# Tasks beside gathered in every second round, up to three in a row, in the bank beside and the first score's two banks

## What is computed

```python
latent_kv = x @ w_kv_down          # 256 -> rank 128
kv = latent_kv @ w_kv_up           # -> keys and values of 16 heads of 64
q = (x @ w_q).reshape(Bx, Tx, 16, 64)
att = jnp.einsum('bqhd,bkhd->bhqk', q, k) * scale
att = jnp.where(causal, att, -jnp.inf)
att = jax.nn.softmax(att, axis=-1)
y = jnp.einsum('bhqk,bkhd->bqhd', att, v)
return y.reshape(Bx, Tx, HD) @ w_out
```

## Time and profile before

| | |
|---|---|
| device time, median of 3 runs | 2116.73 us (2112.48 to 2118.43) |
| span of the profiled execution | 2113.7 us |
| PE busy, share of the span | 1984.7 us, 94% |
| DVE | 1337.2 us, 63% |
| ACT | 1097.9 us, 52% |
| POOL | 1425.9 us, 67% |
| granted clock of TensorE, mean | 0.980 |

### The profile page before, as it was taken

One profiled execution on the slowest core, in us unless ns is written; L12 is line 12 of the kernel. 1 busy time (PEld: TensorE's weight loads), 2 busy tenths in 40 slices (PEclk: granted clock), 3 DMA queues, 4 the chain that ended last, 5 costly groups with the idle time before them and its releaser, 6 DMA issues.

```text
span 2113.7 us, 35206 instructions
## 1 busy us (share of the span) xinstructions
PE 1984.7 (94%) x12886; PEld 1240.9 (59%) x12886; DVE 1337.2 (63%) x2728; ACT 1097.9 (52%) x2236; POOL 1425.9 (67%) x812
## 2 busy tenths in 40 slices
PE   8997788999999999999989999999999999999898
PEld 6775454555655555555555655555555555555466
DVE  7786555576656666666665657576756575656443
ACT  5775543455545454545455444545445445444585
POOL 1333225778687878787857687868786878687822
PEclk9998899999999999999999999999999999999999
DMA  3000000000000000000000000000000000000001
GB/s 124 1 1 1 0 7 13 13 19 10 13 18 16 13 19 12 19 10 19 13 12 17 12 20 11 17 12 20 11 18 11 20 11 18 11 14 11 26 26 60
DMA packets 29243, 37.01 MB, mean 18 GB/s; under 512 B 6928, under 2 KB 20368, under 8 KB 29072
## 3 DMA queue, kind: packets, MB, share of 16 engines
q1 hardware_dynamic: 29072, 34.76, 5.4%
HBM read 30.02 MB, written 4.46 MB: 16 GB/s over the span
## 4 chain that ended last, share of the span: by engine, by line
PE 63%; DVE 14%; POOL 12%; ACT 6%; issue 4%; DMA 1%; POOLq 0%; ACTq 0%; SPq 0%; DVEq 0%
PE heads_out L918 16%; POOL acc L1416 10%; PE beside L723 9%; PE scores L723 7%; PE two_heads L874 7%; PE scores L897 4%; PE scores L903 4%; PE scores L899 4%; PE scores L901 4%; DVE part_max L1112 3%; ACT prob L1331 2%; PE two_heads L723 2%; PE beside L929 2%; PE heads_out L723 1%; DVE wQK_lo L1073 1%
## 5 line engine op out<-in xcount | busy, mean ns | idle before, releaser
L1416 POOL TENSOR_TENSOR acc<-acc,prob 128x1024 f32<-128x1024 f32 (+3 forms) x512 | 1017.9, 1988 | 195.4 <-ACT prob L1331 140.1
L1331 ACT ACTIVATE prob<-scores 128x512 f32<-128x512 f32 (+3 forms) x1280 | 579.4, 539 | 649.2 <-PE scores L903 289.0
L1112 DVE TENSOR_REDUCE part_max<-two_heads 128x2 f32<-128x1024 f32 x384 | 469.3, 1222 | 280.5 <-PE two_heads L874 279.7
L918 PE MATMUL heads_out<-prob,V 128*64 128x512 f32 (+3 forms) x2560 | 544.4, 547 | 0.0
L1109 DVE CUSTOM_DVE_ANT_0 two_heads<-two_heads,mask 128x128 f32<-128x128 f32 (+3 forms) x512 | 242.0, 514 | 180.4 <-PE two_heads L874 180.4
L874 PE MATMUL two_heads<-k_hi,q_hi 64*128 64x512 f32 (+3 forms) x1280 | 274.1, 424 | 62.8 <-DVE part_max L1112 30.6
L918 PEld LDWEIGHTS heads_out<-prob,V 128*64 128x64 f32 x2560 | 156.7, 137 | 232.4 <-issue 209.6
L874 PEld LDWEIGHTS two_heads<-k_hi,q_hi 64*128 64x128 f32 x1280 | 120.6, 184 | 256.6 <-issue 133.4
L897 PE MATMUL scores<-q_hi,k_hi 64*128 64x512 f32 (+3 forms) x1280 | 236.1, 364 | 0.8 <-DVE k_lo L1100 0.5
L903 PE MATMUL scores<-neg_max,sel 64*128 64x512 f32 (+3 forms) x1280 | 235.6, 362 | 0.0
L901 PE MATMUL scores<-q_lo,k_hi 64*128 64x512 f32 (+3 forms) x1280 | 235.5, 362 | 0.0
(11 more groups left out here) (301 smaller groups left out, 2898.7 us busy)
## 6 DMA issues: line engine op xcount, KB each, us to landing
rden<-rden_rows SPq DMA_DIRECT2D x128, 128.0 KB, 2.9
X<-u SPq DMA_DIRECT2D x8, 512.0 KB, 8.7
out<-X SPq DMA_DIRECT2D x8, 512.0 KB, 2.9
wQK_raw<-wQuery SPq DMA_DIRECT2D x16, 192.0 KB, 3.1
wO_raw<-wOut SPq DMA_DIRECT2D x16, 128.0 KB, 2.8
wV_raw<-wValue SPq DMA_DIRECT2D x8, 128.0 KB, 2.9
den<-den_rows SPq DMA_DIRECT2D x64, 4.0 KB
rden_rows<-den SPq DMA_DIRECT2D x64, 4.0 KB, 1.3
```

Source lines behind the costliest of these rows:

```text
L918: made = pe.matmul(heads_out[head(h), x0:], V[vn % NVS][:, tt, p % 2, head(h)], prob[step % NPROB][:, h, x0:], start=t == 0, stop=t == TPB ...
L1112: made = ve.reduce_max(part_max[:, t, :, c:c + 1], two_heads[:, :, 0:width], AX.X)
L1331: ac.activation(prob[step % NPROB][:, h, x0:], bank(task, h)[:, x0:], ACT.Exp).then_inc(empty(task, h)[0], 1)
L1416: po.tensor_tensor(total[:, :, x0:], total[:, :, x0:], new[:, :, x0:], ALU.add).then_inc(acc_ok, 1)
```

## The change

In each round PE's tasks beside were one from any that is open (bank 7), then, in a round with no diagonal step, one more that is due within 8 steps (bank 0), and in rounds with a diagonal step and no denominators one more behind the weighing. Now the rounds alternate. In those with s % 4 == 2 up to three are taken in a row, in banks 7, 0 and 1: any, then one due within 16 steps, then one due within 8. In those with s % 4 == 0 only one that is overdue by two steps or more. None is taken behind the weighing any more. The two projections of a unit are due two steps earlier than they were. What is computed, and by which instructions, stays as it is.

```diff
             if kind == "two_parts":
-                fillers.extend([(s + 2, s + 4 + half, ("project", ready[0][1][1], half)) for half in range(2)])
+                fillers.extend([(s + 2, s + 2 + half, ("project", ready[0][1][1], half)) for half in range(2)])
...
-            filler(10 ** 6)
-            diagonal = not steps[s:s + 2] or any(t >= TPB * UNITS[idx][2] for idx, t in steps[s:s + 2])
-            if not diagonal:
-                self.side_bank = 0
-                filler(s + 8)
+            if s % 4:
+                for n, self.side_bank in enumerate((7, 0, 1)):
+                    filler((10 ** 6, s + 16, s + 8)[n])
                 self.side_bank = 7
+            else:
+                filler(s - 2)
             while self.at < goal - 1:
                 maximum()
...
             due("two_parts")
             due("scale_out")
-            if not due("denominators") and diagonal:
-                filler(s + 8)
+            due("denominators")
```

## The result

The changed kernel takes 2141.78 us (median of 4 runs, 2139.57 to 2143.72), the kernel before, on the same chip, 2114.61 us (4 runs, 2111.7 to 2118.43). The ratio is 1.0134, with a 95% interval of 1.0116 to 1.0152: slower, by 27 us. The forecast was 34 us slower, in a range of 2124 to 2182. The profiled execution of after has a span of 2138.3 us at a mean granted clock of 0.982.

A forecast was written before the change was run, and what follows sets the result against it. PE was taken as the bound, busy 94% of the span. Lost 36 + 33 + 2 = 71, won 22 + 9 + 2 + 3 = 36: +35 us on 2116.7, giving 2151.7, rounded 2151; range 2124 to 2182.

The forecast's parts named there:

- Step 5: Phases 22 and 30: demanded turned maxima and the next task both take bank 7, so PE waits; 33 us lost.
- the forecast's sign: Bank 7 clash would show as L723 waiting for ACT's `neg_max` some 30 times at 1.1 to 1.2 us.
- Step 4: First round of a unit, phases 0, 4, 12, 24: without a task beside, PE idles before the next maximum; 36 us lost.
- Step 2: Phase 6: key gets bank 0, so the denominators no longer wait for bank 7; 9 us won.
- Step 3: Phase 36: no projection behind the weighing, so the next maximum's reduction isn't held back; 2 us won.
- Step 1: Rounds with tasks beside: fewer groups, each costing 0.19 us beyond its products; 22 us won.
- Step 6: Other possible waits: banks 0 and 1, POOL's `oT_lo` (taken as 0), attention's start, batch change and end (+1 us).
- A: Units' first rounds: the lost cover isn't missed, so the kernel is not slower, 2115 us; chance 0.10.
- B: Plain rounds: overdue and demanded tasks fill them, so the change does less, about 2128 us; chance 0.08.
- C: Gathered copies push ACT and POOL behind PE, much slower, 2194 us; chance 0.10.
- The prediction's own side remark: Under the rival that cover isn't missed, if the bank 7 waits were wrong too: 2082 us, and faster.

The follow-up runs named there:

- the banks apart: Changed kernel, but where turned maxima were demanded into bank 7 in a gathering round, the three tasks take banks 0, 1, 7; 2106.99 us.
- The extra work in this round: Changed kernel plus four unread identity transposes into bank 7 in the first round of 56 units; 2145.22 us.
- the key's bank: Kernel before, with only the key of phase 6 put in bank 0 instead of bank 7, from the second pair on; 2099.61 us.
- A group cut in two: Changed kernel, but in phases 14, 18 and 26 the second maximum stands behind the first task beside, making two groups; 2155.04 us, executed once.
- the two kernels with 9.23 and 7.84 us in phase 24: Kernel before (9.23), and kernel before with only the key of phase 6 in bank 0 (7.84), which measured 2099.61 us.
- that in wide rounds: Changed kernel plus the same four unread transposes in 56 plain rounds with a wide weighing (phases 16, 20, 28, 32); 2176.03 us.
- the last kernel of the cover series: Bank-7 clash avoided, any task in units' first rounds except at batch change and end, phase 6 banks ordered 0, 1, 7; 2085.54 us.
- the kernel with cover and late maximum: Bank-7 clash avoided, plus a task in each unit's first round and the second maximum behind the tasks in gathering rounds; 2148.85 us.
- the two kernels with the late maximum: Bank-7 clash avoided, second maximum behind the tasks in gathering rounds from step 24: 2158.8 us; also with a task in units' first rounds: 2148.85 us.

## Why the prediction was right

Its two main losses and its main gain were there, in the rounds that it named and at about their prices. That its total, 34 us, comes so near the 27 measured is in part luck: it missed some 20 us of gains and 7 us of losses, and the gains of step 1 and the losses of steps 4 and 5 came out a little smaller than forecast. By its steps, with what each measured:

- **Step 5**, two tasks in a row in bank 7, forecast 33 us: 31.5 by the banks apart. There are 15 waits in each of the two phases, as many as forecast, and one more in phase 2 of pair 8, behind the change of batch. Phase 22 lost 1.09 us (1.1), phase 30 1.01 (1.2). As idle time the profile shows 0.89 and 0.75 us, not the 1.1 to 1.2 of the forecast's sign, because it counts from the end of the turned maxima and not from where they were issued.
- **Step 4**, the cover of a unit's first round, 36: the gap from the weighing's last product to the next maximum is 0.795 us instead of 0.202, so 0.59 a round (0.60), in phase 0 0.55 (0.55). 46 x 0.59 + 15 x 0.55 = 35. The extra work in this round cost nothing. In the four phases of the step the maxima wait 59 times more, 60 being forecast; 53 in all, since some waits of before in other rounds are gone.
- **Step 2**, 9: 8 by the key's bank, 0.63 in 13 rounds and not 15. What the step missed is the same key's second effect, `wV_lo` behind POOL. After has this gain too (phase 8: 4.87 to 4.15).
- **Step 3**, 2: the gap between scores and maximum in phase 38 is 0.73 us instead of 0.89, 0.16 as forecast.
- **Step 1**, 22: a pair lost 3 x 0.59 + 0.55 + 2.1 = 4.4 us by steps 4 and 5 and was 2.1 longer, so 2.3 were won. Of these the key is 0.6, phase 8 0.35 on the mean (0.7 in every second pair), step 3 0.16, so that some 1.2 are left for fewer groups, 19 us over 15.5 pairs. This is what is left over, not a measurement by itself. The number of groups can be counted in the timelines of PE, and is as forecast: 19 and 15 a pair in before, 10 and 9 in after. In the terms of the step, 0.10 for the first product and 0.09 for leaving, the trace of after has the same rows (0.22, 0.12, 0.21), and across tasks products follow at 0.12. A group cut in two costs 0.4, not 0.19, so the price depends on what stands around it.
- **Step 6** was the term that was mis-sized: +1 for start, change of batch and end. The last pair went from 97.9 to 91.4 us. In before its projections stood in two rounds (phases 24 and 36) in front of an `oT_lo` that wasn't ready, for 3.27 and 3.09 us. Pairs 7 and 10 went from 122.2 and 110.4 to 121.7 and 108.8. Against the 2.1 us of an ordinary pair these three make 8.6 + 2.6 + 3.7 = 15 us better. That is more than the whole gap between forecast and result (35 and 27). Against it stand 3.0 us in the last mixer and 4.2 ahead of the attention, and pair 8, 1.5 longer than an ordinary one. Part of the 15 is the clock: before had four stretches of 3.4 us at the lower level in these three pairs (phase 6 of pair 7, phase 32 of pair 10, phases 24 and 36 of the last), each behind a wait of 2 to 3.3 us, after had none. At the 1.4 us between the two kernels with 9.23 and 7.84 us in phase 24, that is an estimated 6 us of the 15, and whether the new order or the single execution decides on them no run shows. Timeline of PE in before, then its windows with the columns of the earlier trace rows:

```profile
1973.83 0.39 PE L723 MATMUL beside<-wO_hi,oT_hi 128*128 128x256 f32 x1 [3.27 <-POOL oT_lo L1425]
2007.12 0.35 PE L723 MATMUL beside<-wO_hi,oT_hi 128*128 128x256 f32 x1 [3.09 <-DVE oT_lo L1147]
```

```profile
1974.50:1977.90 3.40, 3.40 (x19) 2.47 (x19) 1.38 (x2) 0.13 (x1) 3.23 (x3) 0.50 0.00 0
```

Added up, 35 + 31.5 + 3.0 + 4.2 us were lost and 19 + 8 + 5 (phase 8) + 2 + 15 won: 25, beside 24.6 between the spans. It closes because step 1 is what was left over. The forecast's own sum, 2151.7, stands there as 2151.

**The rivals.** A, the cover isn't missed: fell by the extra work in first rounds (3.4 us) beside that in wide rounds (34.3). B, the change does less: fell by the timeline, plain rounds have no task beside between their maxima and the weighing. C, POOL behind: the wait of `oT_lo` did grow, 107.1 to 126.6 us, but ACT waits for POOL only 28.9, and no row has L917 waiting for `prob`; POOL was never late enough to matter.

The prediction's own side remark, that without both pauses the time would be 2082, comes near the last kernel of the cover series, 2085.5 us, which keeps most of the gathering and has neither pause. That they are so close is luck in part: the cover brought further groups, which the remark leaves out, and it leaves out the gain of step 6 too.

## What to carry to other kernels

Before tasks are gathered for fewer changes of kind (here 0.2 us a group by the rows, 0.4 where one was cut in two), list for each round what they had covered: a round-trip through another engine of 1.7 us with 1.13 of work left in it costs the difference every time. Two tasks in a row need two buffers, and those that a dependency pulls in count as tasks too: look at where the planner puts what is demanded, not only at what the loop chooses. Then put back cover where a pause is, and leave it out where it uses up the tasks that a later wait needs.

## What the runs showed of the hardware

**DVE and POOL shut each other out.** DVE's differences with both inputs in SBUF (`wV_lo`, `wQK_lo`) take 0.41 to 0.42 us for 256 columns when they start first. When a POOL operation is already under way they mostly end 0.28 to 0.29 us after it (128 columns of `wQK_lo`: 0.15 to 0.16 us after it), whatever is left of that: 1.26 to 1.50 us for `wV_lo` before, and the 1.48 of `wQK_lo` in the earlier trace rows, which I had taken for its work; begun ahead of POOL's it takes 0.22 (once, in the kernel with cover and late maximum). It is what made `k_lo` late in step 2. The other way round POOL's `oT` takes 1.41 to 1.56 us instead of 1.28 when DVE's starts with it or at most 0.14 us ahead. The reductions from PSUM (L1112, 1.23 us) are not touched. In the kernel with banks apart POOL starts 0.05 to 0.11 us ahead in phase 8 in four of the pairs, in after behind DVE: a shift of a tenth of a microsecond is worth 0.85 us of the round (4.15 and 5.00). The recorded starts do not always tell who is held up: in the two kernels with the late maximum `wQK_lo` takes its 0.22 us though POOL's `acc` is recorded 0.14 to 0.18 us ahead of it, and it is `acc` that takes 2.59 to 2.65 us instead of 2.38. Why the lead of 0.05 us decides in one case and that of 0.18 in the other is open. The trace books all this as length of the instruction, not as waiting. The Trainium skill, page "SBUF — State Buffer", section "Who interferes with whom", says that a DVE instruction with two SBUF inputs contends with a GpSimd instruction that reads SBUF, that the lock is exclusive, and that the order of issue decides who is blocked. These rows agree with the lock; the order of issue is not in them, only the recorded starts.

**A maximum that waited holds up 128-row products behind it.** From maximum to weighing or task it is 0.31 to 0.33 us when the maximum followed scores without a pause, and 0.42 to 0.43 when it had waited or followed 128-row products. That is a tenth of a microsecond beyond the pause. Where scores follow, as behind the pauses of step 4, it is 0.33 to 0.34 us whether the maximum had waited or not.
